# Key norms summed with time on the partitions, and chunk states stored with time outermost and gathered by ScalarE

## The chip, the cores and the metric

The kernel runs on one core of a Trainium2 chip. The metric is the device time of one execution in microseconds (us), the median of several runs. PE is TensorE's matmul pipe, PEld its weight loads, DVE VectorE, ACT ScalarE, POOL GpSimd, SP the queue from which most transfers are issued. All data are fp32.

## What is computed

One transformer block over x of shape (8, 512, 256): `x + LN(mixer(LN(x)))`, and then `x + LN(ffn(LN(x)))`. The mixer is a recurrence over time with two coupled states per head (32 heads of 16 channels, 32 states each):

```python
dt = clip(softplus(params[..., 0] + dt_bias), DT_MIN, DT_MAX); kd = K_MAX * sigmoid(params[..., 1]); A = exp(A_log)
bc = einsum('bti,oi->bto', value, W_bc).reshape(B, T, H, 4, N)
bc = bc / (sqrt(sum(bc * bc, axis=-1, keepdims=True)) + EPS)
Bz, Bx, Cz, Cx = (bc[..., 0, :], bc[..., 1, :], bc[..., 2, :], bc[..., 3, :])
def step(carry, inp):                      # over the 512 time steps
    S = 1 / (1 + dt * k + dt * dt * A)
    z = S * (z - dt * A * s + dt * (Bz * u));  s = s + dt * z + dt * (Bx * u)
    y = einsum('bhn,bhnd->bhd', Cz, z) + einsum('bhn,bhnd->bhd', Cx, s)
```

Two things of it matter here: the norm of each of the four 32-vectors (per head and time step), and the product of 2x2 matrices over time, per head and state, by which the kernel replaces the step-by-step recurrence.

## The kernel before

Three stages follow each other: `project` (lines 100 to 410: projections, convolution, step sizes; to 240 us), `mix` (lines 415 to 1125: the recurrence; 240 to 2030 us) and `ffn`. `mix` works through 8 rows of the batch in 8 groups of 4 heads each, 64 groups in all. In a group the partitions are 4 heads x 32 states, and the 512 time steps lie in the free dimension as 8 chunks of 64. Each engine runs its own program in a written-out order, and semaphores join them.

PE computes the four vectors of a group two groups ahead (`product`, L670: for each j of 0 to 3, four matmuls of 128x512, each shown as two records), in two PSUM buffers. ACT takes each out with a square (`m_sq`, L822) and a copy (`m_raw`, L823; both in `evacuate`). PE sums the squares over the 32 states of each head (`sum_squares`, L681: `head_sum` is the stationary operand, 512 columns of squares stream). ACT takes the root of all 128x512 sums (`norms`, L831; a table load goes ahead of it). SP gathers the 16 useful rows of the result into the 128x64 tile `compact` (`compact_norms`, L590, four transfers), DVE turns them into reciprocals times the step factors (`scales`, L1002 to L1009), and SP writes them to memory and reads them back spread over all partitions as `m_scale` (`spread_scales`, L597 and L604).

The matrix products over time are `psi`. `step_psi` takes one time step of four groups (a half of the heads) in two DVE instructions of 128x128, `m_prod` (L962) and `m_psi` (L966). Time is innermost in `psi` and `shear`, so the 128 elements of such an instruction lie 65 or 64 elements apart. DVE issues these steps one at a time between the other instructions of a group (`advance(1)`), 32 in each group. The group's other work on DVE begins with `m_raw` times `m_scale` (L1040, L1044), makes `m_k` from `m_raw` and `psi` (L1050 to L1064), then `m_q` (L1069 to L1080), `coef`, the seven dependent steps of X (L1102 to L1113), and the masked scores g (L1119).

PE then waits for `k_ready` and transposes k (`transpose_k`, L715); that point, once per group, is used below as the start of a group on PE. There follow `m_ps_a` for j = 0, the chunk states (L702), the scores (L693), j = 1, sums, j = 2, sums, j = 3, sums and the outputs (L744, L756). ACT's order in a group is: root, copies of k's transpose (`copy_kT`, L837), y with four transfers (L852, L855), `copy_dX` (L844), j = 0, logarithm (`det_log`, L862), `scale_beta` (L812: `shear` times A for the next row), j = 1, j = 2, exponential (`det_inverse`, L868, with its table load), j = 3. In `project`, DVE's `step_sizes` ends at L386, PE's row starts at L229.

## Time and profile before

| | before |
|---|---|
| median of 3 runs | 2361.71 us (2357.69 to 2366.44) |
| the profiled execution | 2356.95 us |
| its span | 2355.2 us |
| PE busy | 2026.4 us (86%) |
| DVE busy | 2053.6 us (87%) |
| ACT busy | 1080.7 us (46%) |
| mean granted TensorE clock | 0.947 of full speed |

The profile is of one execution. The span runs from its first to its last instruction; 1.8 us of the execution's time lie outside it. Busy is the union of an engine's instructions, so two engines near 87% can both be near a limit or take turns. What bounds a stage is read from the windows of that stage.

### The profile page before, as it was taken

How to read it: one execution, taken by the hardware profiler on the slowest of the kernel's cores; microseconds unless marked ns; L12 is line 12 of the kernel's file. 1: busy time of each engine (PE TensorE's matmuls, PEld its weight loads, DVE VectorE, ACT ScalarE, POOL GpSimd, SP SyncE). 2: the span in 40 equal slices, each digit the busy share in tenths (PEclk: the TensorE clock that was granted, in tenths of full speed). 3: DMA queues.
4: the chain of work that ended last, by engine and by line, in shares of the span. 5: the costliest groups of instructions: out<-in, count | busy, mean ns of one | idle time of the engine just before them, and what ended most of it. 6: DMA issues, size and time to landing. Idle time of an engine off the chain costs nothing. (4 is left out here: it accounts for less than half of the span.)

```text
span 2355.2 us, 78715 instructions
## 1 busy us (share of the span) xinstructions
PE 2026.4 (86%) x31266; PEld 1059.6 (45%) x31266; DVE 2053.6 (87%) x5467; ACT 1080.7 (46%) x1700; POOL 83.4 (4%) x28
## 2 busy tenths in 40 slices
PE   6777469999999999899999999998999998357886
PEld 2333124444444444444444544444444444246675
DVE  6887589998999999999989999998999996487774
ACT  4665225544454444445444544444554544024453
POOL 0000000000000000000000000000000000153300
PEclk9898779999999999999999999999999999578997
DMA  4455644565555465545655554655456443443300
GB/s 137 176 212 177 177 93 105 130 143 130 128 129 129 121 142 128 123 106 133 143 128 130 126 128 112 146 132 123 105 131 145 108 97 85 149 160 134 143 27 27
DMA packets 224664, 300.27 MB, mean 127 GB/s; under 512 B 96784, under 2 KB 114192, under 8 KB 218128
## 3 DMA queue, kind: packets, MB, share of 16 engines
q1 hardware_dynamic: 174416, 212.11, 35.8%
q10 hardware_dynamic: 48704, 78.68, 12.9%
q8 instruction: 253, 4.15, 0.8%
q0 software_dynamic: 1152, 4.19, 0.5%
q14 instruction: 139, 1.14, 0.2%
HBM read 240.85 MB, written 50.86 MB: 124 GB/s over the span
## 5 line engine op out<-in xcount | busy, mean ns | idle before, releaser
L670 PE MATMUL m_ps_a<-m_valT,m_w_bc 128*128 128x512 f32 x2048 | 967.1, 611 | 50.4 <-DMA m_valT<-scratch_valT 33.8
L670 PEld LDWEIGHTS m_ps_a<-m_valT,m_w_bc 128*128 128x128 f32 x2048 | 366.8, 191 | 510.0 <-issue 503.6
L822 ACT ACTIVATE m_sq<-m_ps_a 128x512 f32<-128x512 f32 x256 | 152.9, 597 | 540.5 <-PE m_ps_a L670 536.8
L962 DVE TENSOR_TENSOR m_prod<-m_psi,m_shear 128x128 f32<-128x128 f32 x960 | 368.4, 384 | 0.0
L966 DVE TENSOR_TENSOR m_psi<-m_psi,m_prod 128x128 f32<-128x128 f32 x960 | 367.9, 383 | 0.0
L681 PE MATMUL m_ps_s<-m_sq,m_head_sum 128*32 128x512 f32 x512 | 267.9, 606 | 24.4 <-ACT m_sq L822 24.4
L693 PE MATMUL m_ps_g<-m_q,m_k 32*64 32x64 f32 x8192 | 124.8, 234 | 45.0 <-issue 37.2
L693 PEld LDWEIGHTS m_ps_g<-m_q,m_k 32*64 32x64 f32 x8192 | 108.9, 135 | 101.0 <-ACT m_dX L844 55.4
L823 ACT ACTIVATE m_raw<-m_ps_a 128x512 f32<-128x512 f32 x256 | 151.9, 593 | 0.0
L221 PE MATMUL ps_w<-p_xnT,w_in 128*128 128x512 f32 x256 | 119.4, 620 | 16.5 <-ACT gate L284 16.3
L756 PEld LDWEIGHTS m_ps_y<-m_q,m_X 32*16 32x16 f32 x7168 | 103.8, 93 | 53.3 <-issue 53.3
L831 ACT ACT_TABLE_LOAD x64 | 82.1, 1283 | 83.5 <-PE m_ps_s L681 83.4
L844 ACT ACTIVATE m_dX<-m_ps_g 128x128 f32<-128x128 f32 (+1 forms) x128 | 26.8, 261 | 201.0 <-PE m_ps_g L702 181.0
L756 PE MATMUL m_ps_y<-m_q,m_X 32*16 32x64 f32 x7168 | 115.4, 217 | 0.7 <-issue 0.7
L681 PEld LDWEIGHTS m_ps_s<-m_sq,m_head_sum 128*32 128x32 f32 x512 | 35.2, 108 | 178.2 <-issue 145.2
L837 ACT ACTIVATE m_kT<-m_ps_g 128x512 f32<-128x512 f32 x128 | 69.6, 595 | 90.0 <-PE m_ps_g L715 90.0
L1271 POOL TENSOR_TENSOR f_y<-f_y,f_gate 128x2048 f32<-128x2048 f32 x8 | 37.4, 4674 | 2002.0 <-DMA f_svg<-scratch_svgT 1899.9
L1040 DVE TENSOR_TENSOR m_raw<-m_raw,m_scale 128x1024 f32<-128x1024 f32 x64 | 77.3, 1207 | 27.8 <-issue 10.4
L702 PEld LDWEIGHTS m_ps_g<-m_u,m_kT 64*32 64x32 f32 x7168 | 68.1, 106 | 71.3 <-issue 71.2
L744 PE MATMUL m_ps_y<-m_g,m_u 64*16 64x64 f32 x4096 | 86.9, 220 | 15.0 <-issue 7.9
L702 PE MATMUL m_ps_g<-m_u,m_kT 64*32 64x16 f32 x7168 | 76.1, 185 | 21.8 <-issue 20.2
L744 PEld LDWEIGHTS m_ps_y<-m_g,m_u 64*16 64x16 f32 x4096 | 61.2, 94 | 73.1 <-issue 66.7
(143 smaller groups left out, 3085.4 us busy)
## 6 DMA issues: line engine op xcount, KB each, us to landing
m_scale<-scratch_norm SPq DMA_DIRECT2D x256, 256.0 KB, 5.3
m_w_bc<-in_w_bcT ACTq DMA_DIRECT2D x252, 256.0 KB, 3.8
m_shear<-scratch_n_alpha SPq DMA_DIRECT2D x64, 256.0 KB, 5.2
m_shear<-scratch_beta SPq DMA_DIRECT2D x256, 64.0 KB, 3.7
m_det<-scratch_gd SPq DMA_DIRECT2D x256, 64.0 KB, 4.5
scratch_gateT<-gate SPq DMA_DIRECT2D x8, 1024.0 KB, 3.9
scratch_valT<-val SPq DMA_DIRECT2D x8, 1024.0 KB, 4.5
scratch_svgT<-svg SPq DMA_DIRECT2D x8, 1024.0 KB, 5.8
```

What stands on the lines that cost most here:

```text
L221: mm = pe.matmul(ps_w[i % BANKS].ap(), w_in[:, k, col:col + P], xnT[:, k, :], start=(k == 0), stop=(k == KD - 1))
L670: mm = pe.matmul(ps_a[j % 2].ap(), w_bc[:, j, kt, :], valT[:, kt, :], start=(kt == 0), stop=(kt == KI - 1), skip_group_check=True)
L681: pe.matmul(ps_s[j * N:(j + 1) * N, :], head_sum.ap(), sq[:, j % 2, :], start=True, stop=True, skip_group_check=True).then_inc(sums_made.s ...
L693: mm = pe.matmul(ps_g[rows_of(c), h, into], k[s][heads, part, cols], q[s][heads, part, cols], start=(part == 0), stop=(part == 1), skip_gr ...
L702: mm = pe.matmul(ps_dX(c)[h * N:(h + 1) * N, part, :], kT[rows_of(c), part, heads], u[rows_of(c), s, c // 2, h * DH:(h + 1) * DH], start=T ...
L744: mm = pe.matmul(ps_y[h * N:h * N + DH, c * C:(c + 1) * C], u[rows_of(c), s, c // 2, h * DH:(h + 1) * DH], g[rows_of(c), h, c // 2 * C:(c ...
L756: pe.matmul(ps_y[h * N:h * N + DH, cols], X[heads, c - 1, part, :], q[s][heads, part, cols], start=False, stop=(part == 1), skip_group_che ...
L822: act.activation(sq[:, j % 2, :], ps_a[j % 2].ap(), ACT.Square).then_inc(sq_ready.sem, sq_ready.step)
L823: act.activation(raw[s][:, j, :], ps_a[j % 2].ap(), ACT.Copy).then_inc(raw_ready.sem, raw_ready.step)
L831: act.activation(rows_.ap(), ps_s.ap(), ACT.Sqrt).then_inc(norm_ready.sem, norm_ready.step)
L962: dve.tensor_tensor(prod.ap(), psi_t[half][:, :, :, :, t], shear_t[half][:, :, :, t].unsqueeze(1).to_broadcast([P, 2, 2, HALF * NC]), ALU. ...
L966: ins = dve.tensor_tensor(psi_t[half][:, :, :, :, t + 1], psi_t[half][:, :, :, :, t], prod[:, :, ::-1, :], ALU.add)
```

## The change

Norms. `sum_squares` now has the squares as the stationary operand, in four blocks of 128 time steps, and the 4 useful columns of `head_sum` stream; the sums come out with time on the partitions, as 128 x 64 for a group. The root is taken of 128x64 instead of 128x512, and DVE works on it directly: the four gathering transfers (`compact_norms`) are gone. PE transposes the result (`transpose_rows`), ACT copies it (`copy_rows`), and SP stores and spreads it. The three step factors are transposed once per row in `project` (three PE transposes, a 128x384 copy by ACT) and loaded once per row instead of three times per group.

States. `psi` and `shear` have time outermost, so the 128 elements of a step lie side by side. `shear` is loaded into a staging tile and laid out by two ACT instructions per group (`lay_shear`), in place of one. Before `k` is made, ACT copies the group's states, 2080 elements per partition, into a tile `psi_g` with time innermost (`gather_psi`); DVE reads `psi_g`. `k` has one buffer instead of two; `kt` and `kT` share the tile of `scale`.

```diff
+        fac = sb("p_fac", [P, 3 * P])
@@ project: PE, ACT
-                    pe.wait_ge(logit_ready.sem, logit_ready.at(b, -1))
+                    pe.wait_ge(fac_ready.sem, fac_ready.at(b, -1))
...
+                    pe.wait_ge(steps_ready.sem, steps_ready.at(b, 0))
+                    pe.wait_ge(logit_ready.sem, logit_ready.at(b, 0))
+                    for n, v in enumerate((beta, dt, e_inv)):
+                        mm = pe.transpose(ps_l[:, n * P:(n + 1) * P], v.ap(), ident.ap())
+                    mm.then_inc(fac_made.sem, fac_made.step)
...
+                    act.wait_ge(fac_made.sem, fac_made.at(b, 0))
+                    act.wait_ge(fac_stored.sem, fac_stored.at(b, -1))
+                    act.activation(fac.ap(), ps_l[:, 0:3 * P], ACT.Copy).then_inc(fac_ready.sem, fac_ready.step)
@@ mix: tiles
-        psi = sb("psi", [P, 2, 2, HG, NC, C + 1])
-        shear = sb("shear", [P, 2, HG, T])
+        psi = sb("psi", [P, 2, C + 1, 2, 2, HALF * NC])
+        psi_g = sb("psi_g", [P, 2, 2, NC, C + 1])
+        shear = sb("shear", [P, 2, C, 2, HALF * NC])
+        stage = sb("stage", [P, 2, T])
...
-        k = [sb(f"k{s}", [P, 2, T]) for s in range(2)]
+        k = sb("k", [P, 2, T])
...
+        kt = scale[:, 0:2, :]
+        kT = scale[:, 2:4, :]
@@ mix: SP
-                    sp.wait_ge(scaled.sem, scaled.at(b, group - 1))
+                    sp.wait_ge(q_ready.sem, q_ready.at(b, group - 1))
+                    sp.sem_inc(sp_passed, 1)
+                    sp.wait_ge(dX_made.sem, dX_made.at(b, group - 1))
@@ mix: PE
-                    pe.wait_ge(norm_ready.sem, norm_ready.at(b, group - 1))
-                    pe.matmul(ps_s[j * N:(j + 1) * N, :], head_sum.ap(), sq[:, j % 2, :],
-                              start=True, stop=True, skip_group_check=True).then_inc(sums_made.sem, sums_made.step)
+                    pe.wait_ge(rows_copied.sem, rows_copied.at(b, group - 1))
+                    for c in range(TT):
+                        mm = pe.matmul(ps_norm[:, :, j, c], sq[:, j % 2, c * P:(c + 1) * P], head_sum[:, 0:HP],
+                                       start=True, stop=True, skip_group_check=True)
+                    mm.then_inc(sums_made.sem, sums_made.step)
+
+                def transpose_rows(b, group):
+
+                    pe.wait_ge(rows_ready.sem, rows_ready.at(b, group))
+                    pe.sem_inc(passed, 1)
+                    pe.transpose(ps_rows, norm.ap().rearrange("p h j c -> p (h j c)"), ident.ap()
+                                 ).then_inc(rows_made.sem, rows_made.step)
...
                     if ahead:
                         product(b, group + 2, 0, (0, 1, 2))
+                    if more:
+                        transpose_rows(b, group + 1)
@@ mix: ACT
+                def lay_shear(b, group, src, loads=None):
+
+                    cols = slice(group % HALF * NC, (group % HALF + 1) * NC)
+                    dst = [shear[:, group // HALF, :, comp, cols].rearrange("p t c -> p c t") for comp in range(2)]
+                    act.wait_ge(shear_in.sem, shear_in.at(b, (loads or group + 1) * HP - 1))
+                    act.wait_ge(stepped.sem, stepped.at(b - 1, group // HALF))
+                    act.activation(dst[0], chunks(src[:, 0, :]), ACT.Copy, scale=A[:, group:group + 1])
+                    act.activation(dst[1], chunks(src[:, 1, :]), ACT.Copy).then_inc(shear_ready.sem, shear_ready.step)
+
+                def gather_psi(b, group):
+
+                    half, cols = group // HALF % 2, slice(group % HALF * NC, (group % HALF + 1) * NC)
+                    act.wait_ge(stepped.sem, stepped.at(b, group // HALF))
+                    act.wait_ge(raw_used.sem, raw_used.at(b, group - 1))
+                    act.wait_ge(coef_ready.sem, coef_ready.at(b, group - 1))
+                    act.activation(psi_g.ap().rearrange("p r k c t -> p (r k) c t"),
+                                   psi[:, half, :, :, :, cols].rearrange("p t r k c -> p (r k) c t"),
+                                   ACT.Copy).then_inc(psi_ready.sem, psi_ready.step)
...
                         if more:
                             det_inverse(b, group + 2)
+                            gather_psi(b, group + 2)
@@ mix: DVE
+                        dve.wait_ge(psi_ready.sem, psi_ready.at(b, group))
...
+                        dve.tensor_tensor(by_chunk(k.ap()), over_rows_of(r4[:, 0, :]),
+                                          psi_g[:, :, 0, :, 0:C], ALU.mult).then_inc(own.sem, own.one())
```

Three places of the order. The first is ACT in a group of the loop, from the copies of j = 2 to the root. Before, `m_det` with L868 is the exponential, and the copies of j = 3 come next:

```order
L822 ACTIVATE m_sq<-m_ps_a 128x512
L823 ACTIVATE m_raw<-m_ps_a 128x512
L825 DMA m_w_bc<-in_w_bcT 128x512
L867 REGISTER_ALU
L868 ACT_TABLE_LOAD
L868 ACTIVATE m_det<-m_det 128x512
L820 REGISTER_ALU
L822 ACTIVATE m_sq<-m_ps_a 128x512
L823 ACTIVATE m_raw<-m_ps_a 128x512
```

Now, the same place:

```order
L851 ACTIVATE m_sq<-m_ps_a 128x512
L852 ACTIVATE m_raw<-m_ps_a 128x512
L854 DMA m_w_bc<-in_w_bcT 128x512
L903 ACT_TABLE_LOAD
L903 ACTIVATE m_det<-m_det 128x512
L840 ACTIVATE m_psi_g<-m_psi 128x2080
L849 REGISTER_ALU
L851 ACTIVATE m_sq<-m_ps_a 128x512
L852 ACTIVATE m_raw<-m_ps_a 128x512
```

The gather stands between the exponential and the copies of j = 3. The second place is DVE at the start of a group in the loop, now:

```order
L1080 TENSOR_TENSOR m_raw<-m_raw,m_scale 128x1024
L998 TENSOR_TENSOR m_prod<-m_psi,m_shear 128x128
L1084 TENSOR_TENSOR m_raw<-m_raw,m_scale 128x1024
L1003 TENSOR_TENSOR m_psi<-m_psi,m_prod 128x128
L1088 TENSOR_TENSOR m_raw<-m_raw,m_det 128x1024
L998 TENSOR_TENSOR m_prod<-m_psi,m_shear 128x128
L1094 REGISTER_ALU
L1097 TENSOR_TENSOR m_k<-m_raw,m_psi_g 128x1024
L1003 TENSOR_TENSOR m_psi<-m_psi,m_prod 128x128
L1101 TENSOR_TENSOR m_scale<-m_raw,m_psi_g 128x1024
L998 TENSOR_TENSOR m_prod<-m_psi,m_shear 128x128
L1106 TENSOR_TENSOR m_k<-m_k,m_scale 128x1024
```

The product with `m_det` has moved ahead of the two products that make k (before, it stood between them and their sum), and from L1097 to the sum L1106 there are three large instructions and two steps. The third place is PE in a group, from the transposes of k to the products of j = 2, now:

```order
L726 MATMUL m_ps_g<-m_ident,m_k 128x128 x8
L673 MATMUL m_ps_a<-m_valT,m_w_bc 128x512 x3
L693 MATMUL m_ps_s<-m_ident,m_norm 64x128
L714 MATMUL m_ps_g<-m_u,m_scale 32x16 x56
L673 MATMUL m_ps_a<-m_valT,m_w_bc 128x512
L705 MATMUL m_ps_g<-m_q,m_k 64x64 x64
L673 MATMUL m_ps_a<-m_valT,m_w_bc 128x512 x4
L685 MATMUL m_ps_s<-m_head_sum,m_sq 128x4 x4
L673 MATMUL m_ps_a<-m_valT,m_w_bc 128x512 x4
```

The transpose of the norms (L693) is new, and each `sum_squares` (L685) is four matmuls of 4 columns where it was one of 512.

## Rows read from the trace of the kernel before

**Rows 1.** The page: busy time, share of the span and instructions of each engine.
```profile
PE 2026.4 (86%) x31266; PEld 1059.6 (45%) x31266; DVE 2053.6 (87%) x5467; ACT 1080.7 (46%) x1700; POOL 83.4 (4%) x28
```
**Rows 2.** Windows from group start to group start: length, then busy per engine, clock.
```profile
1001.43:1026.86 25.43, 25.02 (x470) 12.14 (x465) 22.67 (x67) 13.35 (x21) 0.00 (x0) 1.00 0.49 120
1026.86:1053.94 27.08, 25.57 (x472) 12.44 (x465) 27.05 (x73) 12.84 (x20) 0.00 (x0) 1.00 0.46 112
1053.94:1081.60 27.66, 25.29 (x467) 12.24 (x465) 26.15 (x71) 12.84 (x20) 0.00 (x0) 1.00 0.68 148
1188.60:1219.00 30.40, 26.81 (x465) 12.70 (x465) 30.37 (x80) 12.12 (x19) 0.00 (x0) 0.94 0.44 103
```
**Rows 3.** The line L715: count: ns min/median/max, first and last start us.
```profile
L715 PE MATMUL m_ps_g<-m_ident,m_k x512: 272/273/477, 325.2 to 2015.1; 128*128 128x128 f32 x171
```
**Rows 4.** Timeline of ACT: the end of three groups' exponentials.
```profile
1017.59 0.60 ACT L822 ACTIVATE m_sq<-m_ps_a 128x512 f32<-128x512 f32 x1 [3.52 <-PE m_ps_a L670]
...
1018.69 1.28 ACT L868 ACT_TABLE_LOAD   x1
1019.99 0.63 ACT L868 ACTIVATE m_det<-m_det 128x512 f32<-128x512 f32 x1
...
1046.14 0.63 ACT L868 ACTIVATE m_det<-m_det 128x512 f32<-128x512 f32 x1
...
1074.72 0.63 ACT L868 ACTIVATE m_det<-m_det 128x512 f32<-128x512 f32 x1
```
**Rows 5.** Timeline of DVE: two of the instructions that make k, with a step between.
```profile
1021.15 1.22 DVE L1050 TENSOR_TENSOR m_k<-m_raw,m_psi 128x1024 f32<-128x1024 f32 x1
1022.28 0.38 DVE L962 TENSOR_TENSOR m_prod<-m_psi,m_shear 128x128 f32<-128x128 f32 x1
1022.58 1.22 DVE L1054 TENSOR_TENSOR m_kt<-m_raw,m_psi 128x1024 f32<-128x1024 f32 x1
```
**Rows 6.** Timeline of PE in one group, and L670 early in the stage.
```profile
281.04 7.13 PE L670 MATMUL m_ps_a<-m_valT,m_w_bc 128*128 128x512 f32 x16
...
1001.43 1.09 PE L715 MATMUL m_ps_g<-m_ident,m_k 128*128 128x128 f32 x8
...
1009.25 3.70 PE L670 MATMUL m_ps_a<-m_valT,m_w_bc 128*128 128x512 f32 x8
1012.88 1.04 PE L681 MATMUL m_ps_s<-m_sq,m_head_sum 128*32 128x512 f32 x2
1013.85 3.70 PE L670 MATMUL m_ps_a<-m_valT,m_w_bc 128*128 128x512 f32 x8
```
**Rows 7.** Timeline of PEld: weight loads of 128 columns.
```profile
1002.25 0.30 PEld L670 LDWEIGHTS m_ps_a<-m_valT,m_w_bc 128*128 128x128 f32 x2
```
**Rows 8.** Groups of DVE instructions by form: busy us, mean ns of one, idle before.
```profile
L962 DVE TENSOR_TENSOR m_prod<-m_psi,m_shear 128x128 f32<-128x128 f32 x960 | 368.4, 384 | 0.0
...
L976 DVE TENSOR_TENSOR m_prod<-m_psi,m_shear 128x64 f32<-128x64 f32 x128 | 28.2, 263 | 13.8 <-ACT m_shear L812 13.8
...
L1009 DVE TENSOR_TENSOR m_compact<-m_compact,m_factor 128x64 f32<-128x64 f32 x64 | 13.8, 216 | 0.4
```
**Rows 9.** Groups of ACT instructions by form.
```profile
L868 ACT ACTIVATE m_det<-m_det 128x512 f32<-128x512 f32 x64 | 40.3, 630 | 27.7 <-DVE m_det L987 27.0
...
L844 ACT ACTIVATE m_dX<-m_ps_g 128x128 f32<-128x128 f32 x64 | 17.7, 277 | 201.0 <-PE m_ps_g L702 181.0 <-issue 20.0
```
**Rows 10.** Timeline of a row's end in the projection stage, all engines.
```profile
175.21 0.29 DVE L386 TENSOR_TENSOR gd<-n_alpha,beta 128x128 f32<-128x128 f32 x1
...
175.54 2.18 PE L229 MATMUL ps_l<-p_xnT,w_in 128*64 128x512 f32 x4
175.65 0.60 ACT L295 ACTIVATE p_u<-ps_u 128x512 f32<-128x512 f32 x1 [0.26 <-PE ps_u L241]
```
**Rows 11.** Timeline of ACT at the start of the mixing stage.
```profile
282.30 2.55 ACT L812 ACTIVATE m_shear<-m_shear,m_A 128x512 f32<-128x512 f32 x4
...
311.39 0.63 ACT L868 ACTIVATE m_det<-m_det 128x512 f32<-128x512 f32 x1 [23.12 <-DVE m_det L987]
```

More of the change, by code:

```diff
@@ L558, in load_val, with load_shear @@
                     sp.dma_start(valT[:, kt, :], dram["valT"][b][:, kt, :]).then_inc(val_in[kt].sem, val_in[kt].step)
[L560 to L561 removed]
+                def load_shear(b, group, dst):
                     for h in range(HP):
[L563 to L569 removed]
+                        sp.dma_start(dst[h * N:(h + 1) * N], spread(dram["shear"][b][:, group * HP + h, :])
+                                     ).then_inc(shear_in.sem, shear_in.step)
                 def load_e_end(b):
@@ L715, in transpose_k, with inner @@
                             mm = pe.transpose(ps_g[:, part, pair * P:(pair + 1) * P],
-                                              k[s][:, part, pair * P:(pair + 1) * P], ident.ap())
+                                              k[:, part, pair * P:(pair + 1) * P], ident.ap())
                         mm.then_inc(kT_made.sem, kT_made.step)
-                def inner(b, group, ahead):
+                def inner(b, group, more, ahead):
                     s = group % 2
@@ L793, in body @@
                             transpose_k(b, group + 1)
-                            inner(b, group + 1, not (last and group >= LAST - 2))
+                            inner(b, group + 1, not (last and group >= LAST - 1), not (last and group >= LAST - 2))
                 over_rows(pe, body)
@@ L871, in _ @@
                 for group in range(HALF):
-                    scale_beta(0, group)
+                    lay_shear(0, group, first_stage[group], HALF)
+                act.wait_ge(shear_ready.sem, shear_ready.at(0, HALF - 1))
                 for j in range(NJ):
@@ L875, in _ @@
                 norms(0, 0)
+                copy_rows(0, 0)
                 for group in range(HALF, HG):
-                    scale_beta(0, group)
+                    lay_shear(0, group, stage)
                 det_log(0, 0)
                 det_inverse(0, 0)
+                gather_psi(0, 0)
                 for j in range(NJ):
@@ L899, in body @@
                             norms(b, group + 2)
+                        if not last and group == 0:
+                            lay_shear(b + 1, 0, stage)
                         if here:
@@ L902, in body @@
                         store_y(b, group)
+                        if more:
+                            copy_rows(b, group + 2)
                         if here:
@@ L908, in body @@
                             det_log(b, group + 2)
-                        if not last and group == 0:
-                            scale_beta(b + 1, 0)
                         if not last and group < LAST:
-                            scale_beta(b + 1, group + 1)
+                            lay_shear(b + 1, group + 1, stage)
                         if ahead:
@@ L935, in _ @@
                     for comp in range(2):
-                        dve.memset(psi[:, row, comp, :, :, 0:1], 1.0 if row == comp else 0.0).then_inc(own.sem, own.one())
+                        dve.memset(psi[:, :, 0, row, comp, :], 1.0 if row == comp else 0.0).then_inc(own.sem, own.one())
                 dve.wait_ge(own.sem, own.n)
@@ L1069, in body @@
                         dve.tensor_tensor(by_chunk(kt), over_rows_of(r4[:, 2, :]),
-                                          psi[:, :, 1, group, :, 1:], ALU.mult).then_inc(own.sem, own.one())
+                                          psi_g[:, :, 1, :, 1:], ALU.mult).then_inc(own.sem, own.one())
                         advance(1)
-                        dve.tensor_tensor(by_chunk(q[s])[:, ::-1], over_rows_of(r4[:, 3, :]),
-                                          psi[:, :, 0, group, :, 1:], ALU.mult).then_inc(raw_used.sem, raw_used.step)
+                        if not (last and group == LAST):
+                            scales(b, group + 1, advance)
+                        dve.tensor_tensor(by_chunk(q[s].ap())[:, ::-1], over_rows_of(r4[:, 3, :]),
+                                          psi_g[:, :, 0, :, 1:], ALU.mult).then_inc(raw_used.sem, raw_used.step)
                         cz_made = own.n
@@ L1092, in body @@
                         advance(1)
-                        if not (last and group == LAST):
-                            scales(b, group + 1, advance)
                         dve.wait_ge(y_made.sem, y_made.at(b, group - 1))
@@ L1115, in body @@
                             dve.wait_ge(X_ready.sem, X_ready.at(b, group * (NC - 1) + c))
+                        if not (last and group == LAST):
+                            log_sum(b, group + 1)
                         for two in range(2):
@@ L1123, in body @@
                             advance(1)
-                        if not (last and group == LAST):
-                            log_sum(b, group + 1)
                         advance(end_at - done)
```

198 lines of the change are left out of this document (93 added, 105 removed).

## The prediction

> **What bounds the kernel now.** I read the page first: PE is busy 86% and DVE 87% of the span, ACT 46% [rows 1]. That names two candidates and decides nothing, so I cut the mixing stage into windows from one start of a group (PE's transposes of k, L715) to the next [rows 2]. A group takes 25.4 to 30.4 us, and in each PE is busy for 25.0 to 26.8 of them; DVE is busy for 22.7 to 27.1 in the usual groups and for all 30.4 in the one at the loop's jump (in both it is what falls into the window, since DVE may run ahead of PE); ACT for 12.8. The reader is to see that PE is nearly full in the shortest group, with DVE a little behind as a second bound. All groups together: from 325.2 to 2015.1 us there are 64 starts [rows 3]; less 1.1 us, since the row gives the last of eight transposes and not the first, 63 intervals take 1688.8 us, **26.8 us each**. The granted clock is 1.00, which is 2.4 GHz, in three of the four windows and 0.94 at the jump.
>
> The third view is ACT's timeline. The exponential of a group ends 19.2, 19.9 and 21.4 us after the group's start (1020.62 against 1001.43, 1046.77 against 1026.86, 1075.35 against 1053.94) [rows 2, 4]. The groups as short as the first are two in eight; I take a mean of 20.0. Nothing of this is late for DVE now: L1050, the first product that makes k, starts at 1021.15 [rows 5] without waiting for ACT.
>
> **The change part by part.**
>
> *The sums on PE.* From one product of eight records to the next are 4.60 us (1009.25 to 1013.85) [rows 6]; 16 records without a sum between take 7.13 us, less about 0.16 of the last one's tail 0.436 each, so eight are 3.49 and a sum with its switches costs 1.11 us. Now it is eight pairs of a weight load of 128 columns and a matmul of 4. Two such loads fit in 0.30 us at a length of 0.19 each [rows 7], so they can start 0.11 us apart: 0.88 us. If they did not overlap it would be 8 x 0.19 = 1.52. The rows show the overlap, so I take 0.88: four sums save 0.9 us per group. The new transpose of the norms gives back about 0.2 (one of L715's eight takes 0.14 [rows 6], and a change of tile shape). PE alone would need 26.8 - 0.7 = 26.1 us.
>
> *The steps on DVE.* 128 elements that lie apart take 384 ns, 64 take 263: 1.89 ns per element. Elements side by side: 64 take 216 ns and 1024 take 1.22 us [rows 5, 8], 1.05 ns per element, which makes 283 ns for 128. 32 steps in each group save 32 x 0.10 = 3.2 us of DVE's 26. The gathering of the norms by SP, and DVE's wait for it, go as well. DVE would need some 23 us: it is no longer a bound, whatever the rest costs.
>
> *The gather on ACT, G.* 2080 elements per partition, read with time outermost. No row has ScalarE reading fp32 elements that lie apart; that is the unknown cost. Below: read side by side, ACT takes 0.63 us for 512 elements out of SBUF and (0.60 - 0.277)/384 = 0.84 ns for each further one [rows 4, 9], so G = 0.63 + 1568 x 0.84 = 1.9 us. Above: at DVE's 1.89 ns per scattered element it is 0.20 + 2080 x 1.89 ns = 4.1 us; at DVE's ratio (1.89/1.05 = 1.8) on ACT's own rate 3.3 us. The only rows on scattered fp32 reads are DVE's, and both read the same memory, so I take the middle of the last two: **G = 3.7 us**.
>
> The Trainium skill bears on this twice, and the two pages point apart. "SBUF — State Buffer", section on the two sides of SBUF, says that the memory has 16-byte lines, that an access pattern needs two hits in a line for full bandwidth and that each move to a new line costs; it ties this to no engine. By that rule the gather, with one element of 4 bytes per line, pays. The trace agrees for DVE: 384 ns against 283 [rows 8]. "ScalarE: Activation LUTs", on ACT_TABLE_LOAD's cost, gives 186 ns and 0.833 ns per element for any function, and names no penalty for strides; by it the gather takes 1.92 us. No row here shows either for ScalarE.
>
> *The loop that the gather closes.* ACT gathers after the exponential, in order, and DVE can't make k before it has `psi_g`, and PE can't begin the next group's transposes before k. From the gather's end: L1097, a step, L1101, a step, L1106. A large one occupies DVE for 1.13 us before a step can start (1021.15 to 1022.28) [rows 5], a step now 0.19, the last large one its full 1.22: 1.13 + 0.19 + 1.13 + 0.19 + 1.22 = 3.86, with two signals of 0.05 us about 3.95. So a group can't be shorter than 20.0 + G + 3.95. What precedes the exponential stays as long as it was: one sum is 0.23 shorter, the norms' transpose is 0.2. At G = 3.7 that is 27.65 us, against 26.1 on PE. PE's second way is as long: the copies of j = 3 wait behind the gather, and its last sum, the outputs and the next start wait for them. In the group at the jump PE's 30.4 - 0.7 = 29.7 stays the longer, 2.05 more in one of eight, 0.26 in the mean. So **27.9 us per group, 1.1 more than now; over 63 intervals +69 us**. DVE's saved 3.2 us turn into waiting for `psi_g`.
>
> Costed at nothing: `lay_shear`'s second instruction and slower writes (up to 2.2 us where 0.7 stood) are covered by ACT's idle time later in the same group, of which the 3.52 us before the copies of j = 2 [rows 4] are the last; without that cover they would add up to 1.5 us to the loop. The spread of the scales may start a little later; DVE's new wait for `psi_g` covers that, and without it each microsecond would delay k.
>
> *Projection.* PE's row starts (L229, 175.54) 0.04 us after `step_sizes` ends (175.50). Now PE waits for that end, three transposes follow, and L229 waits until ACT has copied them, behind its last u copy (175.65 to 176.25) [rows 10]: 0.5 us more, so 176.8, 1.2 us later. By the code DVE's convolution reads what these matmuls make, so seven rows give +8 us (0 to 9).
>
> *Start of the stage.* The first gather stands ahead of the first copies after 311.39, for which PE waits: +3.7. The last four `lay_shear` need a tile loaded in turn, where four scalings took 2.55 us [rows 11]; DVE's first 64 steps, alone there, get shorter. Between 0 and +8, I take +4.
>
> Sum: 69 + 8 + 4 = +81 on the profiled 2357, **2438 us**. The profiled execution is 0.2% under the median of the runs shown, within their spread of 9 us; I add nothing for it.
>
> **Rivals.**
> 1. *No price for scattered reads on ACT: faster.* G = 1.9: the loop is 25.85 and with the jump 26.1, PE 26.1 too; since now one, now the other is longer I take 26.3: 63 x -0.5 = -32, the start +2, projection +8: **2335 us**. The ScalarE page's rule would give this. Against it stand DVE's rows; for it, that they are another engine's. The gain decides at G: at 20.0 + G + 3.95 + 0.26 = 26.8 - 12/63 the two kernels are equal, which is G = 2.4 us; above it the change is slower.
> 2. *Partly paid:* G of 2.2 to 2.9, 24.2 + G per group: 2358 to 2390, centre **2372 us**.
> 3. *The sums' weight loads don't overlap:* four sums cost 6.1 us instead of 3.5. One lies ahead of the exponential, one behind the copies of j = 3, so the loop through PE grows by up to 1.3 us: +80 on the forecast, **2520 us**. The rows of L670 speak against it.
> 4. *The copies by ACT are hidden and DVE was the true bound*, so that DVE's 3.2 us come off: this needs ACT's gather to be early, and ACT's order [rows 4] puts it after an exponential that ends at 20.0. Part of rival 1 at best.
>
> **How the numbers follow.** Forecast (G from 3.0 to 4.4) 0.60, its own range 2400 to 2480; rival 1 0.18; rival 2 0.14; rival 3 and others above 0.08. The range 2330 to 2480 leaves out the lower half of rival 1 and what lies above 2480. A measurement of this kernel tells about 0.5% (12 us) from no change. Faster: rival 1, 0.18, and little else: 0.19. Same (2350 to 2374): half of rival 2 and the edge of rival 1, 0.11. Slower: 0.70.
>
> **What would show it.** Right: L840's mean is 3.3 to 4.1 us; DVE's step groups fall from 384 to about 283 ns, and DVE idles some 4 us per group before L1097, released by ACT's `m_psi_g`; group starts are 27 to 29 us apart; PE idles ahead of the sum of j = 3 or the transposes of k; L685's eight records take 0.9 us. Wrong: an L840 near 1.9 us (then starts near 26 us, and PE full), or starts that are longer than the exponential's end, L840 and 3.95 us added up.

## The result, and the profile after

The changed kernel takes 2514.29 us in the median of 4 runs (2507.04 to 2521.73), the kernel before beside it 2361.93 us: a ratio of 1.067 (95% interval 1.064 to 1.070). The forecast was 2438 us with 2480 as the upper end. The direction was right, the loss of 152 us is twice the forecast one of 76. Of the kernels below, states_mid and early_logits had one execution each far above their others (2993 and 10487 us), which the ratios leave out.

The profiled execution has a span of 2511.3 us. The page gives, where [rows 1] gave 2026.4 for PE and 2053.6 for DVE:

```profile
PE 2121.2 (84%) x32890; PEld 1404.0 (56%) x32890; DVE 1882.3 (75%) x5467; ACT 1394.9 (56%) x1900; POOL 84.0 (3%) x28
```

DVE lost work as intended, and PE is busy for longer than before though its sums became cheaper. Groups by form, and the starts of PE's groups (the line that answers to [rows 3]):

```profile
L998 DVE TENSOR_TENSOR m_prod<-m_psi,m_shear 128x128 f32<-128x128 f32 x960 | 271.7, 283 | 0.0
...
L840 ACT ACTIVATE m_psi_g<-m_psi 128x2080 f32<-128x2080 f32 x64 | 244.1, 3814 | 0.0
...
L831 ACT ACTIVATE m_shear<-m_stage,m_A 128x512 f32<-128x512 f32 x60 | 71.1, 1185 | 13.4 <-DMA m_stage<-scratch_shear 13.4
L832 ACT ACTIVATE m_shear<-m_stage 128x512 f32<-128x512 f32 x60 | 66.1, 1101 | 0.0
```
```profile
L726 PE MATMUL m_ps_g<-m_ident,m_k x512: 272/273/476, 336.8 to 2175.4; 128*128 128x128 f32 x171
```

The steps take 283 ns (forecast 283) and the gather 3.81 us (forecast 3.7). The first group starts at 336.8 instead of 325.2, 11.6 us later (forecast 12). From there to the last group's start at 2175.4 less 1.5 (the row gives its last transpose) 63 intervals take 29.16 us each. Forecast were 27.9, before it was 26.8. So 63 x 2.36 = 149 us are lost in the loop, 12 in front of it, and some 4 come back behind it: the two profiled executions are 156 us apart.

One group on three engines. PE's timeline from its second sum to the next group's start:

```profile
909.43 0.95 PE L685 MATMUL m_ps_s<-m_head_sum,m_sq 128*128 128x4 f32 x8
910.25 3.68 PE L673 MATMUL m_ps_a<-m_valT,m_w_bc 128*128 128x512 f32 x8
913.76 0.95 PE L685 MATMUL m_ps_s<-m_head_sum,m_sq 128*128 128x4 f32 x8
914.64 0.64 PE L757 MATMUL m_ps_y<-m_g,m_u 64*16 64x64 f32 x32
916.90 1.87 PE L685 MATMUL m_ps_s<-m_head_sum,m_sq 128*128 128x4 f32 x8 [1.62 <-ACT m_sq L851]
918.70 3.18 PE L769 MATMUL m_ps_y<-m_q,m_X 32*16 32x64 f32 x112
921.81 1.05 PE L757 MATMUL m_ps_y<-m_g,m_u 64*16 64x64 f32 x32
922.80 1.31 PE L726 MATMUL m_ps_g<-m_ident,m_k 128*128 128x128 f32 x8
```

ACT's timeline in the same stretch:

```profile
912.03 0.63 ACT L903 ACTIVATE m_det<-m_det 128x512 f32<-128x512 f32 x1
912.57 3.80 ACT L840 ACTIVATE m_psi_g<-m_psi 128x2080 f32<-128x2080 f32 x1
...
916.28 0.57 ACT L851 ACTIVATE m_sq<-m_ps_a 128x512 f32<-128x512 f32 x1
```

And DVE's:

```profile
912.76 1.23 DVE L1088 TENSOR_TENSOR m_raw<-m_raw,m_det 128x1024 f32<-128x1024 f32 x1 [0.86 <-ACT m_det L903]
...
916.66 1.23 DVE L1097 TENSOR_TENSOR m_k<-m_raw,m_psi_g 128x1024 f32<-128x1024 f32 x1 [2.47 <-ACT m_psi_g L840]
...
919.34 1.21 DVE L1106 TENSOR_TENSOR m_k<-m_k,m_scale 128x1024 f32<-128x1024 f32 x1
```

k is ready at 920.55 by DVE's rows, 27.2 us after this group's start at 893.40, near the forecast loop. But PE starts the next group only at 922.80. The same sum that took 0.95 us at 913.76 takes 1.87 at 916.90, and the outer outputs take 3.18 us; their 112 matmuls take 1.75 where the clock holds (filler, below). The windows say why (length, then busy per engine; the third number from the end is the granted clock):

```profile
893.40:922.80 29.40, 27.22 (x494) 18.17 (x490) 24.11 (x76) 17.69 (x23) 0.00 (x0) 0.89 0.50 111
340.00:1900.00 1560.00, 1423.64 (x26166) 939.04 (x26164) 1227.85 (x3747) 940.76 (x1227) 0.00 (x0) 0.92 0.50 116
...
905.00:911.50 6.50, 6.50 (x28) 3.88 (x27) 4.98 (x8) 2.93 (x5) 0.00 (x0) 1.00 1.06 214
913.10:916.40 3.30, 2.18 (x42) 1.51 (x40) 1.09 (x2) 3.30 (x2) 0.00 (x0) 1.00 0.34 87
916.60:923.20 6.60, 6.30 (x154) 5.89 (x155) 6.54 (x14) 2.23 (x4) 0.00 (x0) 0.50 0.02 5
```

PE makes a thin sum and the even outputs, waits 1.62 us for the square of j = 3, which ACT makes behind the gather, and then the clock stands at 0.50 (1.2 GHz) until just behind the next group's start. In [rows 2] the clock was 1.00 in all but the jump's group.

### The profile page after: what moved, and what is told of

Its sections match the earlier page's. It is cut to its first block and busy times, and to the rows that moved or that the text cites. A ratio compares the mean times of both kernels' runs of the same rounds, so it can differ in the third digit from the quotient of the medians.

```text
span 2511.3 us, 81935 instructions
## 1 busy us (share of the span) xinstructions
PE 2121.2 (84%) x32890; PEld 1404.0 (56%) x32890; DVE 1882.3 (75%) x5467; ACT 1394.9 (56%) x1900; POOL 84.0 (3%) x28
## 5 line engine op out<-in xcount | busy, mean ns | idle before, releaser
L685 PEld LDWEIGHTS m_ps_s<-m_head_sum,m_sq 128*128 128x128 f32 x2048 | 286.4, 206 | 215.1 <-ACT m_sq L851 122.9
L685 PE MATMUL m_ps_s<-m_head_sum,m_sq 128*128 128x4 f32 x2048 | 272.9, 257 | 112.2 <-ACT m_sq L851 112.2
L1003 DVE TENSOR_TENSOR m_psi<-m_psi,m_prod 128x128 f32<-128x128 f32 x960 | 276.0, 288 | 0.0
L998 DVE TENSOR_TENSOR m_prod<-m_psi,m_shear 128x128 f32<-128x128 f32 x960 | 271.7, 283 | 0.0
L840 ACT ACTIVATE m_psi_g<-m_psi 128x2080 f32<-128x2080 f32 x64 | 244.1, 3814 | 0.0
L872 ACT ACTIVATE m_scale<-m_ps_g 128x512 f32<-128x512 f32 x128 | 71.0, 597 | 235.2 <-PE m_ps_g L726 234.9
L769 PE MATMUL m_ps_y<-m_q,m_X 32*16 32x64 f32 x7168 | 185.2, 288 | 0.2 <-issue 0.2
L1097 DVE TENSOR_TENSOR m_k<-m_raw,m_psi_g 128x1024 f32<-128x1024 f32 x64 | 78.4, 1225 | 141.8 <-ACT m_psi_g L840 132.7
L769 PEld LDWEIGHTS m_ps_y<-m_q,m_X 32*16 32x16 f32 x7168 | 169.2, 132 | 2.0 <-issue 0.9
L1088 DVE TENSOR_TENSOR m_raw<-m_raw,m_det 128x1024 f32<-128x1024 f32 x64 | 78.4, 1225 | 59.2 <-ACT m_det L903 59.0
```

What stands on the lines that cost most here:

```text
L685: mm = pe.matmul(ps_norm[:, :, j, c], sq[:, j % 2, c * P:(c + 1) * P], head_sum[:, 0:HP], start=True, stop=True, skip_group_check=True)
L769: pe.matmul(ps_y[h * N:h * N + DH, cols], X[heads, c - 1, part, :], q[s][heads, part, cols], start=False, stop=(part == 1), skip_group_che ...
L840: act.activation(psi_g.ap().rearrange("p r k c t -> p (r k) c t"), psi[:, half, :, :, :, cols].rearrange("p t r k c -> p (r k) c t"), ACT. ...
L998: dve.tensor_tensor(prod.ap().rearrange("p r k c -> p r (k c)"), psi[:, half, t].rearrange("p r k c -> p r (k c)"), shear[:, half, t].rear ...
L1003: ins = dve.tensor_tensor(psi[:, half, t + 1], psi[:, half, t], prod[:, :, ::-1, :], ALU.add)
```

## Experiments

**The theories.** A: PE's idle wait behind the gather lowers the clock. B: the sums of four columns lower it by themselves. C, formed after the first four runs: thin products and the wait lower it together, neither to this extent alone. D, C's rival: only idle time counts, and a busy PE keeps its clock.

The table holds all runs, each time the median. Ratios are against the kernel before, run beside each; below, "faster" and "slower" by about 1% mean that the 95% interval leaves out 1. The time of a group is (last start - first start)/63; the clock is the mean of 340 to 1900 us; falls are how often in that stretch the trace's record of the granted clock goes from 1.0 to 0.5. From the first start on, the columns are of one profiled execution of each kernel.

| kernel | us | ratio (95%) | first start | us per group | clock | falls |
|---|---|---|---|---|---|---|
| before | 2352.9 to 2361.9 | 1 | 325.2 | 26.8 | 1.00 | 4 |
| changed | 2514.3 | 1.067 (1.064-1.070) | 336.8 | 29.2 | 0.92 | 49 |
| norms_alone | 2379.4 | 1.014 (1.009-1.018) | 335.0 | 27.0 | 0.97 | 20 |
| states_alone | 2476.9 | 1.053 (1.051-1.054) | 339.5 | 28.4 | 0.99 | 8 |
| gather_mid | 2393.0 | 1.016 (1.014-1.018) | 339.8 | 27.3 | 0.96 | 31 |
| filler | 2423.3 | 1.031 (1.027-1.034) | 339.3 | 27.6 | 1.00 | 1 |
| thin_filler | 2768.4 | 1.178 (1.172-1.183) | 339.3 | 32.8 | 0.87 | 51 |
| thin_filler_half | 2527.6 | 1.074 (1.070-1.078) | 341.0 | 29.3 | 0.91 | 54 |
| wide_sums | 2507.9 | 1.065 (1.060-1.071) | 341.2 | 29.1 | 0.93 | 42 |
| mid_wide | 2362.3 | 1.003 (1.001-1.006) | 341.0 | 26.8 | 0.99 | 8 |
| mid_wide_bank | 2357.3 | 1.002 (0.999-1.005) | 334.0 | 26.8 | 0.99 | 8 |
| gather_contig | 2377.6 | 1.011 (1.008-1.015) | 336.7 | 27.0 | 0.97 | 24 |
| states_mid | 2381.8 | 1.011 (1.007-1.015) | 339.4 | 27.0 | 0.99 | 7 |
| early_logits | 2344.4 | 0.995 (0.994-0.997) | 319.6 | 26.8 | 0.99 | 9 |
| all_moved | 2324.0 | 0.986 (0.984-0.989) | 323.5 | 26.4 | 1.00 | 2 |
| norms_best | 2336.9 | 0.993 (0.991-0.996) | 315.2 | 26.7 | 0.99 | 6 |

### One part alone

**norms_alone**: the kernel before with the norms' part of the change only (in the diff, the lines of `project`, `sum_squares`, `transpose_rows`, `copy_rows`, `norm`, `factor`).

> Only the norms' part: sums with the squares as weights and four columns, norms 64 to a partition, transpose back, one load of factors a row. States, their layout and the k and q buffers as before; no gather. Theory A (TensorE's idle wait of 1.6 us for the square of j = 3, behind the gather, is what lowers the granted clock and stretches the last sum and the outer outputs): without a gather there is no such wait, the granted clock stays at 0.99 to 1.00 in the mix as before, DVE stays the bound or PE's 26.1 us does: 26.1 to 26.8 us per group, 2320 to 2375 us in all with 8 us more in the projection. Theory B (the sums of four columns by themselves lower the clock, waits or not): the clock in the mix is 0.90 to 0.95 here too, the outer outputs take over 2 us a group instead of 1.75, and the time is over 2390 us.

**states_alone**: the changed kernel with those lines as before.

> Only the states' part: states time-outermost, the steps on 128 elements side by side, lay_shear, the gather at the end of ScalarE's group, one k buffer, the determinant's product ahead of k. Sums with head_sum as weights over 512 columns, the compact tile and its transfers as before; projection as before. Theory A (the idle wait behind the gather lowers the clock): TensorE waits 1.5 us or more for the square of j = 3 and the granted clock falls as in the changed kernel, 28.8 to 29.6 us per group, 2480 to 2540 us. Theory B (the four-column sums lower it): the wait is there but the clock stays at 0.98 or more, 27.5 to 28.0 us per group by the loop through the gather, 2400 to 2440 us.

Neither theory alone holds. norms_alone has no wait behind a gather and yet 20 falls (before 11 of them PE had been busy without a gap for over 3 us, before the other 9 it had stood idle at some point); states_alone has PE waiting for the square of j = 3 and only 8. Its chain of waits on PE in the loop (line, releaser, us in all, times, longest):

```profile
PE m_ps_s L678 <- ACT m_sq L832: 56.8, 48, 1.2
```

Its waits are 1.2 us and not 1.6, in part since its third sum ends later, so this run differs from the changed kernel in two things. It does show what the gather's loop costs with the clock at 0.99: 28.4 us per group, between the two theories (27.5 to 28.0 by B, 28.8 to 29.6 by A) and 0.75 above the forecast loop of 27.65. In one of its groups the exponential ends 21.5 us after the start (882.3 to 903.79) and not 20.0; whether that accounts for all of it is not shown. Both halves lose time by themselves. That their ratios, 0.014 and 0.053, add up to the whole's 0.067 is partly chance: per group they add up to 1.8 us where the whole loses 2.4, and in the first start to 24 us where the whole loses 12.

### The gather earlier on ACT

```
                             evacuate(b, group + 3, 1, ...)
+                        if more:
+                            gather_psi(b, group + 2)
+                        if ahead:
                             evacuate(b, group + 3, 2, ...)
                         if more:
                             det_inverse(b, group + 2)
-                            gather_psi(b, group + 2)
```

> The changed kernel with ScalarE's gather of the group two on placed between the copies of j = 1 and of j = 2 of the next group, where ScalarE now idles 3.2 us, instead of behind the exponential. Nothing else moves. The exponential then comes some 0.7 us later, and k waits for the determinant's product alone: the loop is 20.0 + 0.7 + 1.2 + 0.3 + 3.95 = 26.2 us against PE's 26.1 us. Theory A: TensorE no longer waits for the square of j = 3, the clock stays at 0.99, 26.2 to 26.8 us per group, 2330 to 2365 us. Theory B (four-column sums lower the clock by themselves): the clock stays at 0.90 to 0.94 in the mix and PE's work is then 27.5 us or more a group, over 2400 us.

121 us come off the changed kernel, and the wait for the square of j = 3 is gone, but not the falls. PE's timeline in a group where it is never idle, and windows of the two stretches:

```profile
855.26 0.95 PE L685 MATMUL m_ps_s<-m_head_sum,m_sq 128*128 128x4 f32 x8
856.14 0.64 PE L757 MATMUL m_ps_y<-m_g,m_u 64*16 64x64 f32 x32
856.71 1.05 PE L685 MATMUL m_ps_s<-m_head_sum,m_sq 128*128 128x4 f32 x8
857.70 2.42 PE L769 MATMUL m_ps_y<-m_q,m_X 32*16 32x64 f32 x112
860.05 1.29 PE L757 MATMUL m_ps_y<-m_g,m_u 64*16 64x64 f32 x32
```
```profile
855.20:858.50 3.30, 3.30 (x107) 3.10 (x109) 3.30 (x6) 2.59 (x4) 0.00 (x0) 1.00 0.30 87
858.70:861.90 3.20, 3.20 (x91) 2.69 (x80) 3.20 (x8) 0.00 (x0) 0.00 (x0) 0.50 0.00 0
```

PE is busy for all 3.30 us, with two sums of four columns around the even outputs, and the clock falls. Of this kernel's 31 falls 22 came like that, behind a PE without a gap. Busy is what the profile's rows say: a sum of four columns is shown as 0.95 us, one of 24 (mid_wide, below) as 0.97, so the rows don't tell how much is streamed in them. That brought theory C.

### Work in the wait

```
                     if more:
+                        for _ in range(8):
+                            pe.matmul(ps_s[:, 2 * P:3 * P], ident.ap(), ident.ap(), start=True, stop=True, ...)
                         sum_squares(b, group + 2, 3)
```

> The changed kernel with eight more products of 128 columns (ident by ident, into 128 unused columns of ps_s, the result is not read) on TensorE just before the last sum of squares, which fill its wait of 1.6 us with work. The gather stays in its place. Theory A (idle lowers the clock): the granted clock stays at 0.98 or more, the outer outputs take 1.75 us, and the loop is the forecast one, 27.5 to 28.0 us per group, 2405 to 2440 us in all: faster with more work. Theory B (four-column sums): the outer outputs still take over 3 us, nothing is gained, 2500 to 2540 us.

More work, and some 90 us faster. Here PE's timeline at the place of the wait, and the window:

```profile
890.30 2.05 PE L785 MATMUL m_ps_s<-m_ident 128*128 128x128 f32 x16
892.18 0.95 PE L685 MATMUL m_ps_s<-m_head_sum,m_sq 128*128 128x4 f32 x8
893.07 1.75 PE L769 MATMUL m_ps_y<-m_q,m_X 32*16 32x64 f32 x112
```
```profile
340.00:1900.00 1560.00, 1486.67 (x28407) 987.51 (x28405) 1294.28 (x3934) 993.53 (x1295) 0.00 (x0) 1.00 0.53 123
```

27.6 us per group with the gather where it was: this is the forecast loop of 27.65 (27.9 with the jump). Its waits between 340 and 1900 us (line, releaser, us in all, times, longest) show that loop: DVE waits for the gather, and PE, whose own work is done in time, for k. In the changed kernel PE waited for k only twice in this stretch.

```profile
DVE m_k L1100 <- ACT m_psi_g L843: 131.9, 55, 2.5
PE m_ps_g L726 <- DVE m_k L1109: 20.2, 49, 0.9
```

But this kernel does not tell C from D; that takes a filler that is busy and thin (`ident[:, 0:HP]` as the moving side). The first, with 16 products, was to take 1.7 us:

> The changed kernel with 16 products of 4 columns (ident by the first four columns of ident, into four unused columns of ps_s, not read) just before the last sum of squares. They occupy TensorE for about 1.7 us as the eight products of 128 columns did, but stream 64 columns instead of 1024. Theory C (the clock follows how much TensorE streams; the four-column sums and the wait behind the gather lower it together, and neither does it alone to this extent): the granted clock falls about as often as in the changed kernel, 0.90 to 0.95 in the mix, the outer outputs take 2.4 us a group or more, 2480 to 2530 us. Theory D (only idle time counts, any product keeps the clock): as with the 128-column filler, clock 1.00, outer outputs 1.75 us, 2405 to 2440 us.

The clock fell 51 times, but the products took 4.7 us a group: a mistake of mine, each is two pairs of weight load and matmul, so its time can't be compared. Half as many are as many pairs as in the filler of 128 columns:

> The 16 products of 4 columns took 4.7 us, not the 1.7 us that was meant (each is two pairs of a weight load and a matmul, 0.107 us a pair at the full clock), so they filled the wait and added to the group. Here there are 8 of them: 16 pairs, 1.7 us at the full clock, the length of the wait of 1.6 us, and as many pairs as the filler of 128 columns has. Only the streamed columns differ between the two. Theory C (what is streamed counts): the clock falls as often as in the changed kernel or oftener, 0.88 to 0.93 in the mix, 2520 to 2620 us, as the pairs themselves get longer at the lower clock. Theory D (being busy is enough): 0 to 5 falls, 2415 to 2440 us as with the filler of 128 columns.

```profile
923.74 0.64 PE L757 MATMUL m_ps_y<-m_g,m_u 64*16 64x64 f32 x32
924.31 1.95 PE L785 MATMUL m_ps_s<-m_ident 128*128 128x4 f32 x16
926.11 1.03 PE L685 MATMUL m_ps_s<-m_head_sum,m_sq 128*128 128x4 f32 x8
927.08 2.31 PE L769 MATMUL m_ps_y<-m_q,m_X 32*16 32x64 f32 x112
```
```profile
340.00:1900.00 1560.00, 1511.19 (x26549) 1036.39 (x26549) 1211.03 (x3696) 929.76 (x1213) 0.00 (x0) 0.91 0.49 115
```

PE is busy for 1511 of 1560 us, more than in any kernel here but thin_filler, and the clock is the second lowest. The two fillers have the same place, the same number of pairs and nearly the same length (1.95 and 2.05 us); with 128 columns the clock falls once, with 4 it falls 54 times. D is out: being busy by the profile's rows does not keep the clock, and before 49 of the 54 falls PE had been busy without a gap for over 3 us. Only the width of the added products differs between these two kernels.

### Wider sums

```
...
-  pe.matmul(ps_norm[:, :, j, c], sq[:, j % 2, c * P:(c + 1) * P], head_sum[:, 0:HP], ...)
+  pe.matmul(ps_sums[:, j, c, :], sq[:, j % 2, c * P:(c + 1) * P], head_sum[:, 0:24], ...)
...
```

The root then reads the first 4 of each 24 columns.

> The changed kernel with the moving side of each sum 24 columns of head_sum instead of 4 (the first four are the heads' sums, the others are not read by the norms), as many weight loads as before. A pair is bound by its weight load, so TensorE's work is as long as it was; only more is streamed. The gather and the wait of 1.6 us stay. Theory C: fewer falls of the clock than the changed kernel's 49 in the mix, the outer outputs nearer to 1.75 us than to 2.6, 2420 to 2480 us. Theory A or D (the wait alone lowers the clock): no change, 2495 to 2530 us.

> The gather between the copies of j = 1 and j = 2, and the sums with 24 columns. With the gather there the clock still fell 31 times in the mix, 22 of them behind 3.4 us in which TensorE was busy throughout with a sum, the even outputs, the last sum and the outer outputs. Theory C: with wider sums at most 10 falls are left, clock 0.99, 26.4 to 26.8 us per group instead of 27.25, 2340 to 2370 us. Theory D: as with the gather moved alone, 2380 to 2400 us.

With the wait in place 24 columns do next to nothing (42 falls; C's 2420 to 2480 us was wrong). With the gather moved they take the falls from 31 to 8 and 31 us off, as C expected, and none of the 8 that are left comes behind a PE that was busy throughout. So both causes must go: wide sums don't make up for the wait, and taking the wait away doesn't make up for sums of four columns.

### The scatter's price, and the states' part with the gather moved

```
-                   psi[:, half, :, :, :, cols].rearrange("p t r k c -> p (r k) c t"), ACT.Copy)
+                   psi[:, half].rearrange("p t r k c -> p (t r k c)")[:, part:part + 4 * NC * (C + 1)], ACT.Copy)
```

> The changed kernel with a gather that reads 2080 elements lying side by side instead of one in 128 (the states it hands on are the wrong ones; amount, place and waits are as they were). Prices the scatter alone. First rival of the prediction: such a gather takes 1.9 us against the 3.8 us measured, so the square of j = 3 comes 1.9 us earlier, TensorE's wait of 1.6 us goes, and so does the wait for psi_g: the loop is 25.9 us, and TensorE decides. With the clock as in the kernel with the gather moved (31 falls) that is 27.0 to 27.5 us per group, 2375 to 2400 us; if four-column sums did not lower the clock, 26.4 us and 2340 us. If the scatter is free (the gather takes 3.8 us here too), 2500 us or more.

```profile
L841 ACT ACTIVATE m_psi_g<-m_psi 128x2080 f32<-128x2080 f32 x64 | 122.9, 1921 | 0.0
```

1.92 us side by side, 3.81 scattered: the scatter doubles it. The figures of the Trainium skill's "ScalarE: Activation LUTs" (What ACT_TABLE_LOAD costs) make an estimate of 1.92 us for 2080 elements, and the run agrees for elements side by side; for scattered ones it is off by 1.9 us, in the direction of the rule on 16-byte lines in the Trainium skill's "SBUF — State Buffer" (SBUF: two separate sides). Yet at G = 1.9 the kernel is still 1.1% slower than before, where rival 1 had it faster: 27.0 us per group with 24 falls, as expected with a lowered clock.

The other run is states_alone with the move of gather_mid:

> The states' part alone (sums over 512 columns and their transfers as before) with the gather moved between the copies of j = 1 and j = 2. It tells how much of the states' part's loss was the gather's place. If all of it: TensorE decides at 26.8 us per group as in the kernel before, the stage starts at 339 us instead of 325, 2365 to 2380 us. If the states' part has another loop (the determinant's product, the scales' transfer), 27.3 us per group or more and over 2400 us.

27.0 us per group, 95 us less than with the gather at the end: the gather's place was most of the states' part's loss. Between its profiled execution and that of the kernel before 25 us are left: 14 by the later first start and 13 in the loop (0.2 us per group), less some 2 behind it. The time expected if the place were all of it, 2365 to 2380 us, was just missed.

### The projection, and k ahead of the exponential

In the projection's steady rows (60 to 250 us) the logits' group of the kernel before was

```profile
L229 PE MATMUL ps_l<-p_xnT,w_in 128*64 128x512 f32 x24 | 12.6, 650 | 0.0
```

and in the changed kernel, with the factors' transposes in front:

```profile
L235 PE MATMUL ps_l<-p_xnT,w_in 128*64 128x512 f32 x24 | 18.7, 927 | 3.6 <-ACT p_fac L309 3.6
L252 PE MATMUL ps_l<-p_ident,beta 128*128 128x128 f32 x7 | 3.0, 427 | 8.0 <-DVE gd L401 8.0
```

PE waits 1.1 us in a row for DVE's steps and 0.6 for the copy, and the logits behind take 927 ns instead of 650. That is the clock: over the logits of the last five rows it was granted at 0.50 to 0.65, in the kernel before at 0.87 to 1.00. Two edits on mid_wide: the transposes go to `ps_u[0]` (mid_wide_bank), and then also the next row's logits ahead of them, with ACT's copy of these logits moved forward alike (early_logits).

```
...
-                    pe.wait_ge(fac_ready.sem, fac_ready.at(b, -1))        # ahead of the logits, in mid_wide_bank
+                    pe.wait_ge(u_ready.sem, u_ready.at(b, TT - 2))        # ahead of the transposes, the same
+                    if not last:
+                        logits_of(b + 1)                                  # early_logits
                     pe.wait_ge(steps_ready.sem, steps_ready.at(b, 0))
                     for n, v in enumerate((beta, dt, e_inv)):
-                        mm = pe.transpose(ps_l[:, n * P:(n + 1) * P], v.ap(), ident.ap())
+                        mm = pe.transpose(ps_u[0][:, n * P:(n + 1) * P], v.ap(), ident.ap())
...
```

> As the run before it in this list (gather in the middle, sums of 24 columns), and in the projection the three transposes for the factors go into the bank ps_u0, when its last tile has been copied, instead of ps_l, so that TensorE's next row of logits waits only for the copy of the logits and no longer for the factors' copy. If that wait is what made the projection 11 to 14 us longer, the states' stage starts 8 to 12 us earlier and the time falls by as much, to 2330 to 2360 us; if it is DVE's steps that wait for the transposes, or the copies on ScalarE, it falls by less than 4 us.

> Gather in the middle, sums of 24 columns, factors' transposes in ps_u0 as in the last run of the call before, and in the projection the logits of the next row are made ahead of the factors' transposes, so that TensorE's wait for DVE's steps (1.1 us in a row) and the slower clock behind it no longer stand in front of the logits. If these two are what is left of the projection's 9 us, the states' stage starts 5 to 8 us earlier than there, 2343 to 2353 us; if not, 2355 to 2360 us.

The first start moves from 341.0 to 334.0 and to 319.6, and in early_logits the group reads

```profile
L235 PE MATMUL ps_l<-p_xnT,w_in 128*64 128x512 f32 x24 | 13.2, 680 | 0.0
```

The bank alone gave 7 us of the 8 to 12 expected, and its ratio (1.002) is not clearly apart from mid_wide's (1.003). With the new order the first start moved by a further 14 us where 5 to 8 were expected: the order is better than that of the kernel before as well. Last, DVE's product with the determinant goes behind k:

```
-  r4[:, 2:4, :] *= det        (waits for det_ready; ahead of the two products that make k)
+  the same, behind the sum that sets k_ready
```

> As early_logits, and on DVE the product with the determinant stands behind k instead of ahead of it, so that k no longer waits for the exponential. TensorE decides the group, so by the argument so far only its 0.1 to 0.2 us of waiting for k goes: 26.4 to 26.7 us per group, 2335 to 2350 us, 3 to 10 us less than early_logits. If DVE's way to k were the bound after all, 20 us or more less.

```profile
L738 PE MATMUL m_ps_g<-m_ident,m_k x512: 269/273/417, 323.5 to 1988.4; 128*128 128x128 f32 x171
```

2324 us, 1.4% faster than before. The edit gave 20 us, more than the 3 to 10 expected from PE's waits for k: 0.4 us per group with 2 falls instead of 9, less a first start 4 us later. In 340 to 1900 us DVE's waits for the exponential (99.8 us, 52 times) are gone, but PE's waits for k fell only from 9.4 to 5.5 us. Per group PE is busy for 24.8 us instead of 25.0 and idle for 1.6 instead of 1.8, so the 0.4 us are about half idle time and half busy time; that the busy half is the fewer falls fits and is not shown by a run.

The last kernel is norms_alone with the edits of wide sums and early_logits, and no others.

> The norms' part alone, with its two flaws mended: sums of 24 columns, and in the projection the factors' transposes in ps_u0 behind the next row's logits. States, shear, k and q as before, no gather. It tells whether the kernel that beat both owes it to the norms' part or to the states' part. Rival 4 of the prediction (DVE is the true bound, its steps of 384 ns): 26.8 us per group as before, the stage starts some 5 us earlier than before or as early, 2345 to 2358 us. If TensorE decides: 26.3 to 26.5 us per group, 2320 to 2340 us, and the states' part adds nothing.

The norms' part alone, mended, gives 0.7% with DVE's steps still at 384 ns; The time of 2336.9 us lies where it was expected if PE decides (2320 to 2340), the 26.7 us per group do not (26.3 to 26.5): they are nearer to rival 4's 26.8. The first start, 10 us earlier than before, gives as much as the loop, and which engine decides in it is not shown. So about half of the final gain is the norms' part with the projection's new order. The rest came only with the states' part, whose gather is off the path, together with the move of DVE's product; no run tells these two apart.

## Why the prediction was off, point by point

- *The sums on PE*: eight records take from 913.76 to 914.64, 0.88 us, as forecast. What was left out is what so thin a sum does to the clock. "PE alone would need 26.1 us" was reckoned at a clock of 1.00; the best measured is 26.4.
- *The steps on DVE*: 283 ns, right; where the prediction sets 384 ns against 283 [rows 8], the 283 was still its own estimate and no row. *The gather*: 3.81 against 3.7 us, right.
- *The loop that the gather closes*: with the clock held it is 27.6 us per group (filler) against a forecast loop of 27.65 and, with the jump, 27.9. Right as a mechanism; 63 x 0.8 = 50 us where 69 were forecast. DVE's wait ahead of L1097 was 2.4 us a time and not some 4, and states_alone, with the same gather in the same place, needs 28.4 us, so the loop's 20.0 us up to the exponential do not hold for every kernel with it.
- *"PE's second way is as long"*: **the step that failed.** I named the wait of the last sum behind the gather and took PE's work behind it at its old durations, so that it fitted under the same 27.65. Measured, the sum, the outer and the odd outputs take 5.9 us (916.90 to 922.80), where the same lines at the full clock take 0.95, 1.75 and 0.64, and so PE's own work, not k, decides when the next group starts. What was wrong is the cost of that work, taken at the full clock. Changed kernel less filler is 1.54 us per group, 63 x 1.54 = 97 us that stand in no term of the sum. [rows 2] had shown a clock of 0.94 in one group, and I read it as a property of the jump.
- *Costed at nothing*: `lay_shear` took 2.3 us (1185 and 1101 ns) and stayed under cover: in the group above ACT still waits 3.24 us for PE ahead of the copies of j = 2.
- *Projection and start*: +11.6 us against +12. PE's first product of the mixing stage comes 8.7 us later (270.0 against 261.3, forecast 8), and 2.9 are added behind it (forecast 4). How it comes about is in part luck: in the projection the wait of 1.1 us in a row for DVE's steps is real, but the slower logits behind it are the clock again, and weren't in the working. And states_alone, with the projection as before, starts 14.3 us later, norms_alone 9.8: the terms don't simply add up, and why is open.
- *Rival 1* had the break-even at G = 2.4 us. gather_contig at 1.92 us is 1.1% slower than before, with 24 falls and a first start 11.5 us later still there. *Rival 2*'s lower end is a slip: by its own rule G = 2.2 gives 26.4 us per group and some 2344 us, not 2358. *Rival 3* is out, the loads overlap. *Rival 4*: what DVE's 3.2 us are worth shows, if at all, only once gather, clock and projection are mended: at most the 0.7% between norms_best and all_moved, and in these the move of DVE's product is counted too.

## What to carry to other kernels

- When an edit turns wide products into narrow ones, or puts a wait of a microsecond or two into PE's stream next to small products, look at the granted clock of that stretch before taking the old durations for the work behind it. A group whose matmuls take twice as long as the same line elsewhere is the sign in the timeline.
- A long instruction added to an in-order engine costs what waits behind it. Put behind the exponential the gather cost 121 us more than in an idle stretch of the same engine 6 us earlier. With the clock held (filler), the late place costs 30 us against gather_mid; the rest is what the clock added.
- Time taken off an engine that is the second bound (DVE's 3.2 us here) can stay unseen until the new waits on the first bound are gone: the whole change was 6.7% slower as it stood and 1.4% faster once mended. Try the mended form before dropping the idea.

## What the runs showed of the hardware

- The granted clock went to 0.50 while PE was busy without a gap: in gather_mid behind 855.20 to 858.50, and in thin_filler_half at 49 of 54 falls. Eight products of 128 columns in a wait of 1.6 us brought it from 0.92 to 1.00 and made the kernel some 90 us faster, though they are pure extra work.
- ScalarE pays for scattered fp32 reads out of SBUF: 3.81 us against 1.92 for 2080 elements per partition. DVE's ratio per element was 1.8 by [rows 5, 8].
